# A decoder's attention on one Trainium2 core: in a head's second step, both halves of the units of maxima ahead of the product with the values

## The reference

```
for each of 16 heads (16 channels each):
    scores = q @ k.T * scale          # 2048 x 2048 (causal) or 2048 x 1601
    scores = masked                   # causal, or a given mask, or none
    attn   = softmax(scores)
    out    = attn @ v
x = layernorm(x + concat(out) @ Wo + bo)
```

## Time and profile before

| | us |
|---|---|
| median of 3 runs | 2905.71 |
| lowest, highest | 2905.32, 2907.97 |
| the profiled execution | 2906.22 |
| span of that execution, first to last instruction | 2904.4 |
| TensorE busy | 2694.6 |
| VectorE busy | 2144.1 |
| ScalarE busy | 1818.8 |
| GpSimd busy | 533.2 |

### The profile page before, as it was taken

How to read it: one execution, slowest core, us unless ns; L and a number is a source line. 1 busy time by engine, 2 the same in 40 slices (tenths; PEclk the granted TensorE clock), 3 DMA queues, 4 the chain that set the end, 5 groups by cost and what they waited for, 6 DMA issues and landing times. The chain is left out here.

```text
span 2904.4 us, 93738 instructions
## 1 busy us (share of the span) xinstructions
PE 2694.6 (93%) x39187; PEld 1018.6 (35%) x39187; DVE 2144.1 (74%) x5870; ACT 1818.8 (63%) x2158; POOL 533.2 (18%) x742
## 2 busy tenths in 40 slices
PE   4999999999999999967999999999999999999998
PEld 1623332432222222233222223563222222266664
DVE  7689998488888888665899995138999999561115
ACT  2278888537777777834588887333888888822222
POOL 0087772020000000001222212303000000002330
PEclk8899999979999999988899999997999999989999
DMA  3456652231100111112111112102122221121112
GB/s 99 121 126 156 132 129 65 91 126 27 26 20 22 27 28 28 29 58 72 41 42 42 43 43 69 36 28 60 26 59 76 57 56 34 38 94 39 41 44 88
DMA packets 122804, 177.26 MB, mean 61 GB/s; under 512 B 38835, under 2 KB 89918, under 8 KB 122128
## 3 DMA queue, kind: packets, MB, share of 16 engines
q1 hardware_dynamic: 103344, 124.55, 16.0%
q0 software_dynamic: 13568, 46.17, 5.8%
q10 hardware_dynamic: 5472, 0.56, 0.2%
HBM read 131.75 MB, written 31.96 MB: 56 GB/s over the span
## 5 line engine op out<-in xcount | busy, mean ns | idle before, releaser
L801 DVE TENSOR_REDUCE mpart<-ps 128x1 f32<-128x512 f32 x1536 | 979.1, 683 | 77.5 <-PE ps L598 74.0
L598 PE MATMUL ps<-stack 48*32 48x512 f16 (+6 forms) x13312 | 969.0, 350 | 59.1 <-DVE mpart L801 14.3
L523 ACT ACTIVATE xT<-ps,exp_scale 128x1024 f32<-128x1024 f32 (+3 forms) x800 | 793.2, 1029 | 233.3 <-PE ps L619 106.6
L523 ACT ACTIVATE cn<-ps,exp_scale 128x1024 f32<-128x1024 f32 (+4 forms) x800 | 741.3, 959 | 173.0 <-PE ps L619 75.4
L619 PE MATMUL ps<-stack 50*32 50x512 f16 (+3 forms) x11648 | 747.9, 372 | 31.5 <-ACT xT L523 23.5
L598 PEld LDWEIGHTS ps<-stack 48*32 48x32 f16 x13312 | 287.5, 90 | 1040.2 <-DVE mpart L801 515.8
L794 DVE CUSTOM_DVE_ANT_0 scrap<-ps,arena 128x401 bf16<-128x401 f32 (+1 forms) x1024 | 527.1, 573 | 90.3 <-PE ps L598 90.3
L668 PE MATMUL ps<-xT,vall 128*17 128x512 f32 (+4 forms) x3648 | 414.5, 514 | 2.3 <-POOL xT L482 1.9
L668 PE MATMUL ps<-cn,vall 128*17 128x512 f32 (+3 forms) x3392 | 408.4, 501 | 1.2 <-ACT cn L523 1.0
L619 PEld LDWEIGHTS ps<-stack 50*32 50x32 f16 x11648 | 196.8, 90 | 188.1 <-ACT xT L523 95.6
L788 DVE CUSTOM_DVE_ANT_0 scrap<-ps,scrap 128x128 bf16<-128x128 f32 (+3 forms) x512 | 247.6, 484 | 17.4 <-PE ps L598 12.1
(11 more groups left out here) (291 smaller groups left out, 2696.2 us busy)
## 6 DMA issues: line engine op xcount, KB each, us to landing
stack<-q_parts SPq DMA_DIRECT2D x384, 64.0 KB, 2.9
stack<-k_parts SPq DMA_DIRECT2D x192, 64.0 KB, 3.0
wbuf<-in_maskT POOLq DMA_DIRECT2D x48, 256.0 KB, 4.7
arena<-in_moe_w SPq DMA_DIRECT2D x19, 512.0 KB, 4.7
stack<-k_parts SPq DMA_DIRECT2D x192, 50.0 KB, 2.3
stack<-sums_inverse SPq DMA_DIRECT2D x16, 512.0 KB, 5.7
parts<-osb SPq DMA_DIRECT2D x240, 32.0 KB
wbuf<-in_mask POOLq DMA_DIRECT2D x16, 401.0 KB, 4.3
```

What stands on the lines that cost most here:

```text
L523: nc.scalar.activation(e.prob[tile % P_SLOTS][0:rows, half * HALF + first:(half + 1) * HALF], S_PS(g)[0:rows, first:HALF], ACT.Exp, scale= ...
L598: last = nc.tensor.matmul(bank[quarter(j), i * w:i * w + w], qs[b][rows, at:at + 32], ks[b][rows, a:a + w], start=True, stop=True)
L801: nc.vector.tensor_reduce(dst, src, AX, ALU.max).then_inc(unit_used, 1)
```

## The change

In step n = 1 of a head (not of head 0) `middle` is the number of all units of the step, not half of them rounded up. So one unit of the step moves from behind `product` to ahead of it; in the second phase it moves ahead of `mask_scores` as well. All else is as before.

```diff
                         turned = h + (1 if n <= turn else 2)
                         now = range(before[n], share[n]) if turned < H else range(0)
-                        middle = -(-len(now) // 2)
+                        middle = len(now) if n == 1 and h else -(-len(now) // 2)
                         for u in now[:middle]:
                             unit(turned, u)
                         if masked and h * ns + n + 2 < H * ns:
                             mask_scores(h + (n + 2) // ns, (n + 2) % ns)
                         if slots[n][5]:
                             product(h, n)
                         for u in now[middle:]:
                             unit(turned, u)
```

## The result

| | before | after |
|---|---|---|
| median of 4 runs, us | 2905.5 | 2927.3 |
| lowest, highest | 2905.1, 2908.0 | 2921.2, 2934.4 |
| the profiled execution, its span | 2906.2, 2904.4 | 2921.2, 2919.4 |

The changed kernel is slower: ratio 1.0074, interval 1.0047 to 1.0101. That is 22 us in the median where 4 were forecast, outside the range and outside the 0.2% that was called no change. And it no longer repeats: its executions lie 13 us apart. Mean granted clock of TensorE and time go together: 0.957 in the executions of 2921 and 2923 us, 0.954 in those of 2931 and 2934. The profile shown is of the fastest of the four, so what the slower ones had beyond it stands in no trace.

What follows compares the result with a forecast made beforehand. A loop between TensorE and VectorE was taken to bound each head. Phase costs 3.5 + 1.1 + 0.6 - 1.1 = 4.1 us on the median of 2905.7 gave 2909.8 us, range 2903 to 2920.

Steps and rivals of the forecast that it cites:

- The copy: Before the product of step 1: its wait for the copy gives no gain, at most 0.5 us in 3 places.
- The order, phase by phase: Heads 1 to 14, cost per phase: second 3.5 us, fourth 1.1, first 0.6, third a gain of 1.1.
- Rows 2's window of 39.50 us: Profile window of one second-phase head, taken to stand for the fourteen changed heads; 39.75 us was forecast after the change.
- The product's delay: Product of step 1 starts later behind the moved unit: 0.48, 0.50, 0.60, 0.61 us in first, second, third, fourth phase.
- The walk through the second phase: Second phase, step 1: product 0.50 us late, 0.25 stay per head after VectorE's unit in hand; 3.5 us in all.
- at full clock: All four attention phases: TensorE shows busy for 95 to 97% at full clock.
- (d): No wait for the copy to fill; the slip goes into TensorE's idle time, 0.36 us per head: 2905.7 us, chance 0.20.
- (a): Nothing is returned: each head loses its product's whole delay, 31 us in all: 2936 us, chance 0.05.
- (b): Less is returned than worked out behind the late product: 9.8 us in all, 2915.5 us, chance 0.27.
- (c): VectorE's idle time behind the product is gone for good, heads get shorter by 12 us in all: 2893.5 us, chance 0.06.
- 0.62 on no change: Whole kernel: chance that the time stays within 0.2%, 5.8 us, of before; the forecast (0.42) and (d) (0.20) together.

Runs made afterwards that it cites:

- the filled kernel: The change in all four phases, with the unit ahead of the moved one issued twice, against the kernel before: 2913.1 us, ratio 1.0017.
- the late product's run: The kernel before, no unit moved, but step 1's product in heads 1 to 14 also waits for the next piece's exponential: 2949.1 us, ratio 1.014.

## Why the prediction was wrong, point by point

**The copy.** Right. The waits for the copy are still 0.5 us in 3 places:

```profile
  ACT osb L496: 0.5, 3
```

**The order, phase by phase.** Right within 0.03 us per head:

| | before | forecast | after, undisturbed |
|---|---|---|---|
| first | 24.36 | +0.04 | 24.38 |
| second | 39.02 | +0.25 | 39.25 |
| third | 24.09 | -0.08 | 23.98 |
| fourth | 32.50 | +0.08 | 32.55 |

Fourteen of each make 2.7 us, where the sum had 4.1. Rows 2's window of 39.50 us was, to 0.06, the tenth head of the phase. That one lasts 39.44, since VectorE has more work in it (34.13 us, 33.33 in the others), and 39.66 in the changed kernel. So it could not stand for the fourteen, and the 39.75 announced is 0.5 too long for most heads; the difference is what counts. The product's delay came as worked out in all four phases: 0.47, 0.49, 0.60 and 0.59 us, with 0.48, 0.50, 0.60 and 0.61 forecast. The walk through the second phase holds step by step, seen in the head whose copy starts at 718.16 and ends at 718.75:

```profile
719.54 0.84 PE L598 MATMUL ps<-stack 48*32 48x401 f16 x8
720.05 0.55 PE L647 MATMUL ps<-arena,big 64*32 64x512 bf16 x8
720.53 1.05 PE L668 MATMUL ps<-cn,vall 128*17 128x512 f32 x8
721.52 0.41 PE L619 MATMUL ps<-stack 50*32 50x512 f16 x8
721.74 0.35 PE L598 MATMUL ps<-stack 48*32 48x401 f16 x8
...
722.14 0.58 DVE L794 CUSTOM_DVE_ANT_0 scrap<-ps,arena 128x401 bf16<-128x401 f32 x1 [0.67 <-PE ps L598]
```

The product starts 1.78 us after the copy's end (1.8 were announced, 1.29 before), the first new unit 0.22 after the scores, VectorE 0.40 after that; its idle time has moved from behind the product to one unit later, 0.45 having become 0.67.

**The step that failed** is in the first paragraph: "at full clock" was read as a property of the phases and then kept in every term of the sum. I priced what waits behind the late product and never what the gap does to TensorE itself: no term, and no rival, has a fall of the clock. I had even counted TensorE's idle times as a cushion, in rival (d). The profile shows what a fall costs, 1.57 us a head, five times in 15.0 us, and the filled kernel that the gap is behind more than half of the loss: with the same order and the same lateness of the product, the loss goes from 12 us (ratio 1.0041) to 5 (1.0017), the size of the sum. How the 22 us of the first median divide isn't known beyond the 15.0 of its fastest execution. The Trainium skill, TensorE: Matmul & The Clock Gate, A second HAM failure mode: psum-queue depth-cycling, tells of TensorE idling briefly for PSUM banks between groups of matmuls and of its clock swinging between the two levels for that. The prediction drew on that page for its rule on order, and not on this one. The moved unit waiting for its bank looks like that case, and the trace agrees as far as it goes, with 0.20 us of idle time in front of the unit at 2258.00; heads with the same wait and no fall show that it isn't the whole rule.

**The rivals.** (a) fell: a delay is lost whole only if no unit moves (the late product's run). (b) named the right side and the wrong cause. (c) fell: VectorE's idle time came back one unit later. (d) was right that there is no wait to fill and wrong that the slip goes into idle time.

**The chances.** 0.62 on no change rested on a spread of 3 us in three runs. In the later series the kernel before itself spreads over 14 us in 23 runs and over 12 in 27.

**Still open**: what decides in which head the clock falls. In the changed kernel TensorE waits 0.20 us at the moved unit in the third and fourth phase, where the falls are, and less where none is: 0.15 in the second and 0.08 in the first. But the late product's first phase, with 0.55 us, has no fall either. Open too: what the 3 us outside the heads depend on; why the first four executions of the changed kernel reached 2934 and the next five stayed at 2922.

## What to carry to other kernels

Where TensorE is close to always busy, a wait that is moved on its queue can have two prices: what stands behind it, and the engine's own clock. The first can be worked out from the bank that the moved instruction needs; for the second, compare heads or iterations of equal work, and look at the granted clock of each one that is longer. A wait ahead of an instruction that used to be covered by a long matmul stream is best left under that stream.

## What the runs showed of the hardware that I had not expected

The granted clock fell, in some heads and not in others with the same waits, at idle times of a few tenths of a microsecond in a stretch in which TensorE is busy for 95%: 0.20 us at the moved unit, 0.57 us ahead of the late product. Each time some 3.4 us went by at 1.2 GHz; that cost 1.57 us at the moved unit and 1.1 to 1.2 at the late product. Falls came back in up to six heads running, at the same place, while a head with a fall lasted as long as the falls lay apart. And four redundant matmuls at each of the 56 moved units made the changed kernel faster: 2913.1 against 2922.2 us.
